# Softmax attention on one core: max products issued in twos, score products in threes and ones around the value products

## The reference

```
q, k, v = (proj(Wq), proj(Wk), proj(Wv))        # 16 sequences, 16 heads, 512 tokens, 16 features a head
q, k = _apply_rope(q, k, cos, sin)
scores = jnp.einsum('bhqd,bhkd->bhqk', q, k) / jnp.sqrt(jnp.float32(dk))
attn = jax.nn.softmax(scores, axis=-1)
out = jnp.einsum('bhqk,bhkd->bhqd', attn, v)
out = out.transpose(0, 2, 1, 3).reshape(B, S, D)
return out @ Wo.T
```

## Time and profile before

| | |
|---|---|
| median of 3 runs | 2708.31 us (2702.72 to 2710.55) |
| profiled execution | 2699.52 us, of which the span of the core is 2697.9 us |
| max products of `attention_mix` | from 259.68 us to 1079.72 us of the span |
| busy over the span | PE 90%, DVE 64%, ACT 47%, POOL 42% |
| mean granted clock of TensorE | 0.946 of full |

### The profile page before, as it was taken

How to read it: one execution, slowest core, us unless ns; L and a number is a source line. 1 busy time by engine, 2 the same in 40 slices (tenths; PEclk the granted TensorE clock), 3 DMA queues, 4 the chain that set the end, 5 groups by cost and what they waited for, 6 DMA issues and landing times. The chain is left out here.

```text
span 2697.9 us, 47073 instructions
## 1 busy us (share of the span) xinstructions
PE 2424.7 (90%) x14506; PEld 1332.6 (49%) x14506; DVE 1739.1 (64%) x3661; ACT 1266.7 (47%) x2564; POOL 1128.3 (42%) x1350
## 2 busy tenths in 40 slices
PE   8996899999999999799889993899999979898885
PEld 5653133333333333266557662566666556556663
DVE  7996888888888888188422222688888759632221
ACT  3553477666767767444223230555555424322221
POOL 6888100000010000133236663677777713226765
PEclk9998799999999999899989995999999989998998
DMA  5555332333323331155848862011111036766883
GB/s 167 187 180 172 107 95 87 91 94 91 98 83 94 91 89 56 50 176 184 256 137 227 204 148 55 13 39 38 37 37 33 21 116 203 234 190 185 202 203 53
DMA packets 289375, 325.31 MB, mean 121 GB/s; under 512 B 28945, under 2 KB 270753, under 8 KB 289185
## 3 DMA queue, kind: packets, MB, share of 16 engines
q1 hardware_dynamic: 257536, 274.49, 33.6%
q0 software_dynamic: 27136, 46.16, 8.5%
q10 hardware_dynamic: 4512, 2.40, 0.4%
HBM read 217.23 MB, written 105.19 MB: 120 GB/s over the span
## 5 line engine op out<-in xcount | busy, mean ns | idle before, releaser
L720 ACT ACTIVATE a_probs<-a_ps_s 128x512 f32<-128x512 f32 x1024 | 537.0, 602 | 284.7 <-PE a_ps_s L597 272.4
L672 DVE TENSOR_REDUCE a_row_max<-a_ps_m 128x2 f32<-128x1024 f32 x512 | 607.6, 1219 | 89.6 <-PE a_ps_m L571 85.4
L597 PE MATMUL a_ps_s<-a_qs,a_ks 98*128 98x512 bf16 (+1 forms) x1024 | 319.5, 391 | 8.6 <-ACT a_probs L720 7.3
L612 PE MATMUL a_ps_o<-a_probs,a_va 128*32 128x512 f32 x2048 | 273.2, 606 | 0.8 <-ACT a_o_sb L729 0.8
L1538 POOL TENSOR_TENSOR b_spread<-b_decay,held_own_sb 128x512 f32<-128x512 f32 x256 | 269.3, 1086 | 8.2 <-DVE b_weight L1636 8.2
L571 PE MATMUL a_ps_m<-a_ks,a_qs 48*128 48x512 bf16 x1024 | 207.2, 402 | 17.2 <-DVE a_row_max L672 11.5
L546 POOL DMA_DIRECT2D x<-a_xo x32 | 23.5, 734 | 437.3 <-DVE a_xo L705 437.3
L571 PEld LDWEIGHTS a_ps_m<-a_ks,a_qs 48*128 48x128 bf16 x1024 | 49.3, 93 | 311.2 <-issue 191.0
L1636 DVE TENSOR_TENSOR b_weight<-b_ps_s,b_spread 128x512 f32<-128x512 f32 x256 | 163.8, 682 | 17.6 <-PE b_ps_s L1773 17.6
L597 PEld LDWEIGHTS a_ps_s<-a_qs,a_ks 98*128 98x128 bf16 (+1 forms) x1024 | 76.2, 97 | 166.9 <-ACT a_probs L720 75.5
L517 POOL CAST a_high<-a_row_max 128x32 bf16<-128x32 f32 x32 | 6.7, 209 | 320.2 <-DVE a_row_max L672 320.2
(11 more groups left out here) (350 smaller groups left out, 5273.7 us busy)
## 6 DMA issues: line engine op xcount, KB each, us to landing
parts<-a_parts SPq DMA_DIRECT2D x16, 1536.0 KB, 6.2
a_qs<-parts SPq DMA_DIRECT2D x384, 64.0 KB, 2.2
a_ks<-parts SPq DMA_DIRECT2D x384, 64.0 KB, 2.2
rows<-m_early SPq DMA_DIRECT2D x32, 640.0 KB, 3.2
m_early<-x SPq DMA_DIRECT2D x32, 512.0 KB, 4.0
m_own<-in_L_ffn_w_gate_dram SPq DMA_DIRECT2D x24, 384.0 KB, 4.3
m_own<-in_L_ffn_w_up_dram SPq DMA_DIRECT2D x24, 384.0 KB, 5.7
m_own<-in_L_ffn_w_down_dram SPq DMA_DIRECT2D x24, 384.0 KB, 6.6
```

What stands on the lines that cost most here:

```text
L597: nc.tensor.matmul(s_bank(name, step)[:], ks[u][0:K_ALL[e], h, t * P:(t + 1) * P], qs[u][0:K_ALL[e], h, :], start=True, stop=True).then_in ...
L612: last = nc.tensor.matmul(ps_o[VW * j:VW * (j + 1), :], va[n.u][:, t, (h0 + j) * VW:(h0 + j + 1) * VW], probs[:, group % 2, j, t, :], star ...
L672: nc.vector.tensor_reduce(row_max[:, n.k // 4 % 2, t, :, n.p % 4], m_bank(name, step)[:], AX.X, ALU.max).then_inc(m_drained, 1)
L720: nc.scalar.activation(probs[:, group % 2, j, t, :], s_bank(name, step)[:], ACT.Exp, scale=DK ** -0.5).then_inc(s_drained, 1)
```

## The change

PE's list is put in another order. Before, a step was max0, score0, score1, output, mix1, shift, max1, score2, score3, max2, score4, score5, mix0, max3, score6, score7. Now it is max0, max1, score0, score1, score2, output, mix1, score3, shift, max2, max3, score4, score5, score6, mix0, score7. `M_ORDER`, the list of DVE and that of ACT follow. Nothing is computed otherwise.

```diff
-    M_ORDER = [("max0", 0, 1, 0), ("output", L_OTURN, 2, 1), ("shift", L_TURN, 4, 3), ("max1", 0, 1, 0), ("max2", 0, 1, 0), ("max3", 0, 1, 0),
+    M_ORDER = [("max0", 0, 1, 0), ("max1", 0, 1, 0), ("output", L_OTURN, 2, 1), ("shift", L_TURN, 4, 3), ("max2", 0, 1, 0), ("max3", 0, 1, 0),
...
-            walk_pairs(pe, [(0, max_products(0)), (L_S, scores(0)), (L_S, scores(1)), (L_OTURN, turn_output), (L_MIX + 1, mix_values(1)),
-                            (L_TURN, turn_shift), (0, max_products(1)), (L_S, scores(2)), (L_S, scores(3)), (0, max_products(2)), (L_S, scores(4)), (L_S, scores(5)), (L_MIX, mix_values(0)),
-                            (0, max_products(3)), (L_S, scores(6)), (L_S, scores(7)),
+            walk_pairs(pe, [(0, max_products(0)), (0, max_products(1)), (L_S, scores(0)), (L_S, scores(1)), (L_S, scores(2)), (L_OTURN, turn_output),
+                            (L_MIX + 1, mix_values(1)), (L_S, scores(3)), (L_TURN, turn_shift), (0, max_products(2)), (0, max_products(3)),
+                            (L_S, scores(4)), (L_S, scores(5)), (L_S, scores(6)), (L_MIX, mix_values(0)), (L_S, scores(7)),
                             (L_ATT[0], turn_att(0)), (L_ATT[1], turn_att(1)), (L_OUT[0], project(0)), (L_OUT[1], project(1))])
...
-            walk_pairs(dve, [(0, maxima(0)), (L_OTURN, normalise), (L_TURN, copy_shift), (0, maxima(1)), (0, maxima(2)), (0, maxima(3)),
+            walk_pairs(dve, [(0, maxima(0)), (0, maxima(1)), (L_OTURN, normalise), (L_TURN, copy_shift), (0, maxima(2)), (0, maxima(3)),
...
-            walk_pairs(act, [(L_S, exponentials(0)), (L_S, exponentials(1)), (L_OCOPY, copy_output)]
-                       + [(L_S, exponentials(i)) for i in range(2, 8)] + [(L_ATT[0], copy_att(0)), (L_ATT[1], copy_att(1))])
+            walk_pairs(act, [(L_S, exponentials(i)) for i in range(3)] + [(L_OCOPY, copy_output)]
+                       + [(L_S, exponentials(i)) for i in range(3, 8)] + [(L_ATT[0], copy_att(0)), (L_ATT[1], copy_att(1))])
```

## The result

The changed kernel takes 2729.58 us (median of 11 runs, 2716.20 to 2742.66), the kernel before 2708.31 (2696.07 to 2723.83): a ratio of 1.0068, 95% interval 1.0041 to 1.0094. It is slower by 0.7%; 2726 us was predicted. A ratio is not quite the quotient of the medians, which are of all executions.

What follows compares the result with a forecast made beforehand. PE's list of stages was taken as the bound, DVE close second. Per eight steps, waits of 3.2 us against 1.8 saved gave +1.4; with the early steps +18 us, so 2708.3 becomes 2726 us, 8-in-10 range 2712 to 2744.

Steps and rivals of the forecast that it cites:

- the eight: Eight attention steps, read from max0 of step 40 to max0 of step 48: 53.0 us predicted instead of 51.6.
- Max behind max 0.22, passages from five to four, a half step of 2.62: On PE, a second max costs 0.22 us and a passage 0.10; a half step falls from 2.72 to 2.62.
- the rival's, 25 us under before: Faster rival: the ring's waits are hidden and only saved passages count, -25 us, 2683 us; chance 0.07.
- Plain half step, 2.84 against 2.84, no wait: The next half's max1 needs a buffer free after 2.84 us; PE arrives at 2.84, so no wait.
- the second part of the slower rival: Each of some 11 plain half steps per eight steps waits 0.05, 8 us more; chance 0.15 with its first part.
- Output, wait 0.48: PE reaches the output 1.23 us behind max0, whose buffer is free at 1.71: wait 0.48, net +0.40 without an out.
- Out, 0.72 and then 0.12: Max1 behind an out waits 0.72 us for the residual, then the output 0.12 more; net +0.67 each.
- Shift, 0.61: Max3 behind a shift waits 0.61 us for the shift's buffer, emptied by the cast; net about +0.53 each.
- Steps 16 to 127, +19.6: Fourteen times eight steps, each +1.4 us from waits of 3.2 against 1.8 saved: +19.6 us.
- Steps 8 to 15, +0.5, and steps 6 and 7, -1.1: Steps 8 to 15, with no out, lose 0.5 us; steps 6 and 7, at clock 0.50, save 1.1 in passages.
- the shift's term: At the one shift in steps 0 to 5, POOL's split lies behind two reductions instead of one: about -1.0 us.
- No change within 0.3% (the turn hidden by the three scores): Rival: three scores ahead of the mix let ACT catch up at loop turns, 8 us back; centre 2713, chance 0.13.

Runs made afterwards that it cites:

- e3: The changed kernel with output and out moved into the scores' ring, the shift ahead of mix1 and the output behind it; ratio 0.992 to the kernel before.
- e6: e3's kernel with scores in twos, the shift behind mix0 and the output between score2 and score3; ratio 0.9891 to the kernel before.
- e10: e6's kernel run once more, unchanged, beside e9; ratio 0.9866 to the kernel before.
- e7: The changed kernel with DVE taking each maximum over the first 256 of 512 keys only; 2710.83 us in one run.
- e2: The changed kernel with scores in twos around the mix instead of threes and ones, max stages still in twos; 2756.32 us, ratio 1.0147 to the kernel before.
- e1: The changed kernel with only the shift moved, to directly behind mix1 instead of behind score3; 2728.69 us in one run.
- e5: The kernel before with e3's rings, the output moved behind mix1 and the shift behind score5; ratio 1.0018 to the kernel before.
- e4: The kernel before with the shift moved behind score5 and the output behind mix0, rings left alone; ratio 1.0024 to the kernel before.
- e9: e3's kernel with the shift moved behind mix0, scores still in threes and ones, the output behind mix1; ratio 0.9947 to the kernel before.
- e8: The kernel before with DVE taking each maximum over the first 256 of 512 keys only; 2700.38 us in one run.

## Why the prediction was right

By its own steps, the eight first (predicted 53.0, measured 53.14). The terms of the sum, put to the steps 40 to 47 in which they stand, are +0.23, +0.20, -0.20, +0.47, +0.23, +0.47, -0.20 and +0.20. The steps took 6.13, 6.46, 7.21, 6.54, 7.82, 6.01, 5.44, 6.01 and take 6.31, 6.67, 7.01, 7.03, 8.10, 6.50, 5.30, 6.23, a change of +0.17, +0.21, -0.21, +0.49, +0.28, +0.49, -0.14 and +0.21. So every term is met where it belongs, not only in the total:

- *Max behind max 0.22, passages from five to four, a half step of 2.62*: right. The second max stage comes 0.23 behind the first, the half step is 2.61. The rule of the Trainium skill, page "TensorEngine Tiling (Array Packing)", section "Key Properties", that changing the tiling mode drains the array, agrees with these 0.10 us a passage. A time like the rival's, 25 us under before, came only with e3, e6 and e10 (19, 25 and 34 us by their medians), in which the output and the out no longer share the max stages' ring.
- *Plain half step, 2.84 against 2.84, no wait*: right in the main. Of the 64 plain half steps from step 24 on that have no turn in them, 38 take 2.61, 12 take 2.63 and one 2.65; 13, the second half of step 6 of each eight, take 2.67, over the 2.65 that the prediction set as a sign of failure. The 0.05 lies ahead of a third score (0.27 where 0.22 is its pace), that is, by its place, at a bank that ACT empties and not at a max buffer; the prediction had put ACT's waits at nothing. At under 0.1 an eight it weighs about 1 us, and the second part of the slower rival, 8 us, didn't come.
- *Output, wait 0.48*: the output starts 1.71 behind max0, as worked out. (Before, where no out stands in between, its buffer was that of max3 of the step ahead, with one max stage and four scores between them, not two as "The change" has it.) It stands 1.17 behind the first of its three scores; without a wait, in e7, it is 0.66, so PE waits 0.51. e2 (+0.23 for a score less) and e7 (gone with half a reduction) show that it is this wait.
- *Out, 0.72 and then 0.12*: max1 stands 0.94 behind max0 (predicted 0.94; of 26 places 14 have 0.85 or 0.86, six 0.94, six 1.04 or 1.05), and the output is at 0.81 behind three scores, late by 0.12 (529.85 to 530.66, where 0.69 is the pace).
- *Shift, 0.61*: max3 stands 0.84 behind max2 in 14 of 26 places and 0.93 or 0.94 in 12; predicted 0.83. In the rows shown the cast starts 0.72 behind the shift, where the sum had 0.63. e1 shows that the distance is fixed.
- *Steps 16 to 127, +19.6*: +20.5 (728.9 to 749.4) up to the last max3, +21.8 up to the start of step 127. The pace was thus mis-sized by 2.2: 1.51 an eight for 1.4 is 1.5 in all, and the turns are 1.2 dearer, which together more than make it up.
- *Steps 8 to 15, +0.5, and steps 6 and 7, -1.1*: mis-sized too. Steps 8 to 15 took 49.44 and take 47.90; TensorE's granted clock went from 0.50 to 1.00 at 304.0 us instead of 309.7. The order of PE has no part in it that I could show: e6 and e10 are one kernel, their clock rose at 301.6 and 306.2 us, and these eight steps took 44.83 and 46.25. Over all twelve kernels the rise lies between 296.6 and 309.7 us, and these steps take 44.8 to 49.4, longer in the main where it comes late. Steps 0 to 7 gave 1.27 and not 2.1: the shift's term held (0.94, predicted 1.0), but steps 6 and 7 gave 0.33 for 1.1. So the start gave 2.8 us where the sum had 1.6. The two misses, 2.2 and 1.2, have opposite signs and partly cancel: +18 was predicted, +19.0 is measured up to the start of step 127 (and 17.7 for the stretch, which ends earlier in its step). That the sum came this near is in part luck; the eight, 1.51 against 1.4, is not.
- *No change within 0.3% (the turn hidden by the three scores)*: fell. The six turns cost 1.2 to 1.5 us, 1.0 to 1.3 before.

Windows of before and after the clock's rise, of the kernel before and then of the changed kernel:

```profile
304.00:309.60 5.60, 5.60 (x19) 0.81 (x18) 3.21 (x4) 2.17 (x4) 0.00 (x0) 0.50 0.11 36
309.80:316.00 6.20, 6.20 (x38) 1.54 (x36) 5.26 (x5) 4.81 (x10) 0.00 (x0) 1.00 0.12 43
```

```profile
301.00:307.00 6.00, 5.56 (x26) 1.52 (x24) 5.25 (x5) 3.68 (x8) 0.46 (x2) 0.75 0.12 33
```

In a window over the rise the changed kernel shows 0.75, half of it at either level; the kernel before is still at 0.50 there. The last out ends 18.9 us later than before, and the span is 22.1 longer: the other 3.2 lie in layers that the change doesn't touch, and one execution of each can't say why.

## What to carry to other kernels

When stages share a ring of buffers, write down for each stage the distance at which its buffer comes free (fill, wait in the emptying engine's own list, emptying), and compare it with PE's own work in between: grouping like products shortens the work and leaves the distance; here waits of under 0.2 us, or none, became waits of 0.5 to 0.8. A grouping pays when the stages that stand alone (an output, a shift) are first given a buffer or a place with slack; here this turned +0.7% into -1.1% (e6) and -1.3% (e10). And a wait of the weight loader is no wait of the array: rank waits by the products' own rows.

## What the runs showed of the hardware that I had not expected

In some executions the granted clock fell from 1.00 to 0.50 (the lower of its two levels, 1.2 GHz) for some 3.4 us right behind a turn of the loop, inside the attention. Windows of e6 (us, busy of PE, PEld, DVE, ACT, POOL; clock) and PE's timeline:

```profile
545.00:550.00 5.00, 3.86 (x23) 0.87 (x21) 3.16 (x4) 2.85 (x6) 0.66 (x3) 1.00 0.23 56
...
550.70:554.00 3.30, 3.30 (x15) 0.83 (x14) 1.62 (x3) 1.07 (x3) 0.00 (x0) 0.51 0.00 0
554.20:560.00 5.80, 5.80 (x39) 1.92 (x39) 5.26 (x7) 4.43 (x9) 0.00 (x0) 1.00 0.25 73
```

```profile
548.89 0.39 PE L620 MATMUL a_ps_s<-a_qs,a_ks 98*128 98x512 bf16 x1 [1.14 <-ACT a_probs L741]
...
550.36 0.39 PE L620 MATMUL a_ps_s<-a_qs,a_ks 112*128 112x512 bf16 x1 [0.22 <-ACT a_probs L741]
550.67 1.92 PE L635 MATMUL a_ps_o<-a_probs,a_va 128*32 128x512 f32 x8
```

PE had stood 1.14 us behind ACT at the turn, then the mix took 1.92 where it takes 1.06. A turn with such a dip costs 2.8 to 3.6 us, without one 0.8 to 2.0. e5 had dips at all six turns, e4 and e7 at four, e6 and e9 at two, and e10, the same kernel as e6, at none; before, the change, e1, e2, e3 and e8 had none either. In e5's traced execution this is the whole of the missing gain: 14 x (51.33 - 51.63) is -4.2 us, its turns are dearer by 12.7 in all, which makes +8.5, and its stretch is 7.3 longer than before. That execution was the slowest of ten (2734.02 us, median 2715.13), so how often the dips come in the others isn't shown; their mean granted clock, 0.939 to 0.945, is lower than that of the kernel before beside them (0.941 to 0.948, the one left out aside), which fits dips in them too. A dip always came behind a stretch in which PE idled at the turn, but PE idles at every turn, and the turns without one are not clearly cheaper in the kernels that had none (0.8 to 1.7 us) than in the others (1.3 to 2.0); what decides in one execution and not in the next stays open; no run shortened a turn.
